# Attention output kept transposed up to the output projection, with the softmax division moved into the feed stage

## The reference, cut to what matters

```python
h = layernorm(x) * (1 + ca) + sa
q = h @ W_q;  k = h @ W_k;  v = h @ W_v
latent = (k + v) @ W_down_kv
k_rec, v_rec = latent @ W_up_k, latent @ W_up_v          # split in 16 heads
scores = q k_rec^T / 16 * exp(-0.01 |i - j|)
attn = softmax(scores);  out = attn @ v_rec              # heads joined to 256
x = x + ga * (out @ W_o)
h = layernorm(x) * (1 + cb) + sb
x = x + gb * fp4_linear(silu(fp4_linear(h, w_gate)) * fp4_linear(h, w_up), w_down)
```

## Time and profile before

| what | value |
|---|---|
| median of 3 runs | 2783.0 us (2781.36 to 2785.18) |
| span of the profiled execution, first to last instruction | 2775.7 us |
| PE / DVE / ACT / POOL busy, share of the span | 94% / 85% / 58% / 35% |
| mean granted TensorE clock | 0.940 of full |
| attention ends, feed setup ends, last instruction, about | at 2077, 2118 and 2776 us |

### The profile page before, as it was taken

How to read it: one execution, slowest core, us unless ns; L and a number is a source line. 1 busy time by engine, 2 the same in 40 slices (tenths; PEclk the granted TensorE clock), 3 DMA queues, 4 the chain that set the end, 5 groups by cost and what they waited for, 6 DMA issues and landing times. The chain is left out here.

```text
span 2775.7 us, 54634 instructions
## 1 busy us (share of the span) xinstructions
PE 2597.7 (94%) x15110; PEld 1209.7 (44%) x15110; DVE 2345.5 (85%) x4659; ACT 1601.3 (58%) x2988; POOL 970.2 (35%) x865
## 2 busy tenths in 40 slices
PE   5887679999999999999999999999978999999998
PEld 3333213343444444344344344443323566666665
DVE  5888698888888888888888888888756999999997
ACT  3666507777777777777777777777762222222221
POOL 3666522122122122122122122122231555555654
PEclk8767659999999999999999999999997999999999
DMA  4777864446455455455456455456201111111110
GB/s 152 246 247 255 265 129 73 71 74 99 62 85 87 63 82 82 71 78 86 70 78 86 72 80 86 69 79 94 39 11 38 37 41 40 40 40 42 40 32 18
DMA packets 207121, 238.56 MB, mean 86 GB/s; under 512 B 32256, under 2 KB 150784, under 8 KB 206720
## 3 DMA queue, kind: packets, MB, share of 16 engines
q1 hardware_dynamic: 194560, 218.56, 40.7%
q0 software_dynamic: 3072, 8.39, 1.2%
q10 hardware_dynamic: 9216, 8.39, 0.9%
HBM read 149.79 MB, written 83.89 MB: 84 GB/s over the span
## 5 line engine op out<-in xcount | busy, mean ns | idle before, releaser
L856 DVE CUSTOM_DVE_ANT_0 unread<-max_ps,toeplitz_sb 128x1024 bf16<-128x1024 f32 x1024 | 1219.2, 1219 | 230.5 <-PE max_ps L689 221.9
L817 ACT ACTIVATE probs<-score_ps 128x512 f32<-128x512 f32 x2048 | 1113.3, 597 | 438.3 <-PE score_ps L722 299.7
L689 PE MATMUL max_ps<-k_low,q_low 96*128 96x512 bf16 x2048 | 717.5, 393 | 30.0 <-DVE ident_bf L847 17.9
L651 POOL TENSOR_TENSOR probs<-probs,up_probs 128x512 f32<-128x512 f32 x256 | 336.8, 1316 | 624.4 <-ACT up_probs L821 624.4
L750 PE MATMUL pv_ps<-probs,v 128*32 128x512 f32 x4096 | 548.9, 608 | 3.4 <-POOL probs L651 3.4
L722 PE MATMUL score_ps<-q_low,k_low 99*128 99x512 bf16 (+3 forms) x1280 | 407.9, 320 | 4.9 <-ACT probs L817 4.1
L714 PE MATMUL score_ps<-q_up,k_up 99*128 99x512 bf16 (+3 forms) x1280 | 408.0, 319 | 4.5 <-ACT probs L817 3.8
L1284 PE MATMUL gu_ps<-wgu_t,turned 128*128 128x512 f32 (+1 forms) x768 | 314.7, 559 | 0.6 <-DVE hid L1445 0.6
L657 POOL DMA_DIRECT2D attn<-out_n x64 | 48.8, 762 | 698.3 <-DVE out_n L920 674.8
L714 PEld LDWEIGHTS score_ps<-q_up,k_up 99*128 99x128 bf16 x1280 | 123.8, 97 | 350.4 <-ACT probs L817 325.2
L689 PEld LDWEIGHTS max_ps<-k_low,q_low 96*128 96x128 bf16 x2048 | 194.0, 99 | 156.5 <-DVE row_max L856 83.9
(11 more groups left out here) (145 smaller groups left out, 3218.2 us busy)
## 6 DMA issues: line engine op xcount, KB each, us to landing
splits<-parts SPq DMA_DIRECT2D x128, 384.0 KB, 2.6
q_low<-splits SPq DMA_DIRECT2D x192, 128.0 KB, 4.4
k_low<-splits SPq DMA_DIRECT2D x192, 128.0 KB, 7.0
q_up<-splits SPq DMA_DIRECT2D x192, 128.0 KB, 9.4
k_up<-splits SPq DMA_DIRECT2D x192, 128.0 KB, 12.0
v_padded<-v_out SPq DMA_DIRECT2D x64, 256.0 KB, 3.5
v<-v_padded SPq DMA_DIRECT2D x32, 512.0 KB, 13.9
x_in<-in_L_attn_x SPq DMA_DIRECT2D x16, 512.0 KB, 4.6
```

Of the source, the lines that this page charges most:

```text
L651: nc.gpsimd.tensor_tensor(probs[:, g % PROBS, :, at:at + P], probs[:, g % PROBS, :, at:at + P], up_probs[:, g % 2], ALU.add).then_inc(diag ...
L689: mm = pe.matmul(max_ps[:, i % 2, half * HALF:(half + 1) * HALF], low[0][u][0:KROWS, h, qb * P:(qb + 1) * P], low[1][u][0:KROWS, h, half * ...
L817: nc.scalar.activation(probs[:, g % PROBS, h, :], score_ps[:, i % 2, :], ACT.Exp).then_inc(exp_done, 1)
L856: nc.vector.tensor_tensor_reduce(unread[:, i % 2, :], max_ps[:, i % 2, :], toeplitz[:, at:at + S], 1.0, -3.0e38, ALU.mult, ALU.max, row_ma ...
```

## The change

The attention output is no longer transposed and divided in the attention stage. ACT copies a finished half to one of two halves of `out_t`, and SP (not POOL) stores its 4 heads and its row sums, five DMAs, to `attn_t` (head, feature, token) and `sums`. `turn_out`, `invert_sums`, `normalise` and POOL's store go. In the feed setup the sums of all tokens are loaded, inverted on DVE in one operation over 128 x 1024 elements and stored to `inverse`. In the feed stage each tile loads its transposed attention (one DMA), the inverse sums spread over 16 feature rows each (two DMAs) and x; POOL multiplies the first two (`normalise_attention`, 128 x 256); PE projects the result directly. `turn_attention` goes, and ACT copies only the transposed input, 256 wide. PE's turning of the input waits only for its own buffers.

```diff
@@ attend_stage
-    out_t = sb("out_t", [P, HALF], F32)
-    inv_sum = sb("inv_sum", [P, DIAG, UH], F32)
-    out_n = sb("out_n", [P, DIAG, UH, HD], F32)
+    out_t = sb("out_t", [P, 2, HALF], F32)
...
+        def store_out(b, u, hf):
+            n = 2 * (UNITS * b + u) + hf
+            sp.wait_ge(out_copied, n + 1)
+            for h in range(UH):
+                sp.dma_start(t["attn_t"][b, u * UH + h, :, hf * HALF:(hf + 1) * HALF],
+                             out_t[h * VW:h * VW + HD, hf, :]).then_inc(out_stored[hf], 16)
+            sp.dma_start(t["sums"][b, u * UH:(u + 1) * UH, hf * HALF:(hf + 1) * HALF],
+                         out_t[HD:P:VW, hf, :]).then_inc(out_stored[hf], 16)
...
                 load_up(b if u < UNITS - 1 else b + 1, (u + 1) % UNITS)
+            if not (isinstance(unit, int) and unit == 0):
+                store_out(b if u > 0 else b - 1, (u - 1) % UNITS, 1)
+            store_out(b, u, 0)
+            if not (last and u == UNITS - 1):
                 load_max_rows(unit + 1, (u + 1) % UNITS)
...
-        def store(b, u, hf):
-            n = 2 * (UNITS * b + u) + hf
-            pool.wait_ge(out_ready, n + 1)
-            pool.dma_start(t["attn"][b, hf * HALF:(hf + 1) * HALF, u * UH * HD:(u + 1) * UH * HD].rearrange(
-                "(c p) n -> p c n", p=P), out_n[:].rearrange("p c h d -> p c (h d)")).then_inc(out_stored, 16)
...
-            if g == TILES + DIAG:
-                pe.wait_ge(out_ready, 2 * unit + 1)
+            if g == TILES + DIAG and not last:
+                pe.wait_ge(max_turn_copied, unit + 2)
...
-        def turn_out(n, turned_maxima=0):
...
-            for c in range(DIAG):
-                mm = pe.transpose(side_ps[:, c, :], out_t[:, c * P:(c + 1) * P], w["ident"][:])
-            mm.then_inc(out_turned, 1)
...
-        def copy_out(n):
-            act.wait_ge(pv_done, TILES * (n + 1))
-            act.wait_ge(out_turned, n)
-            nc.scalar.activation(out_t[:], pv_ps[:], ACT.Copy).then_inc(out_copied, 1)
+        def copy_out(unit, hf):
+            act.wait_ge(pv_done, TILES * (2 * unit + hf + 1))
+            if not (isinstance(unit, int) and unit == 0):
+                act.wait_ge(out_stored[hf], 16 * OUT_STORES * unit)
+            nc.scalar.activation(out_t[:, hf, :], pv_ps[:], ACT.Copy).then_inc(out_copied, 1)
...
-            nc.vector.reciprocal(inv_sum[:], turned[:, :, :, HD]).then_inc(inv_ready, 1)
...
-            nc.vector.tensor_tensor(out_n[:], turned[:, :, :, 0:HD],
-                                    inv_sum[:].unsqueeze(3).broadcast_to([P, DIAG, UH, HD]),
-                                    ALU.mult).then_inc(out_ready, 1)
@@ feed_setup_stage
+        sp.dma_start(sums[:], t["sums"].rearrange("b h s -> (b h) s")).then_inc(sums_loaded, 16)
         sp.dma_start(wo[:], t["wo"].rearrange("(k p) n -> p k n", p=P)).then_inc(wo_loaded, 16)
+        sp.wait_ge(sums_inverted, 1)
+        sp.dma_start(t["inverse"].rearrange("b h s -> (b h) s"), inverse[:]).then_inc(inverse_stored, 16)
+        sp.wait_ge(inverse_stored, 16)
...
+        dve.wait_ge(sums_loaded, 16)
+        nc.vector.reciprocal(inverse[:], sums[:]).then_inc(sums_inverted, 1)
+
         dve.wait_ge(wo_loaded, 16)
@@ feed_stage
-            sp.dma_start(attn_in[i % 4][:], t["attn"][b, i * P:(i + 1) * P, :]).then_inc(tile_loaded[i % 4], 16)
+            sp.dma_start(attn_in[i % 4][:], t["attn_t"][b, :, :, tokens].rearrange(
+                "(k h) d s -> (h d) k s", k=DC)).then_inc(tile_loaded[i % 4], 16)
+            heads = H // DC
+            for k in range(DC):
+                sp.dma_start(inverse_in[i % 4][:, k, :], t["inverse"][b, k * heads:(k + 1) * heads, tokens].unsqueeze(
+                    1).broadcast_to([heads, HD, P])).then_inc(tile_loaded[i % 4], 16)
             sp.dma_start(res_in[i % 4][:], t["x"][b, i * P:(i + 1) * P, :]).then_inc(tile_loaded[i % 4], 16)
...
-            pe.wait_ge(turned_copied, n + 1)
+            pe.wait_ge(attn_ready, n + 1)
             pe.wait_ge(x1_ready, n)
             for k in range(DC):
-                mm = pe.matmul(out_ps[:, 0:D], turned[i % 2][:, k, :], w["wo_g"][:, b, k, :],
+                mm = pe.matmul(out_ps[:, 0:D], attn[i % 2][:, k, :], w["wo_g"][:, b, k, :],
...
-        def turn_attention(b, i):
...
+        def normalise_attention(b, i):
+            n = TILES * b + i
+            count = held(pool, 16 * LOADS * ((TILES // 4) * b + i // 4 + 1))
+            if not (isinstance(b, int) and n < 2):
+                pool.wait_ge(projected, n - 1)
+            pool.wait_ge(tile_loaded[i % 4], count)
+            nc.gpsimd.tensor_tensor(attn[i % 2][:], attn_in[i % 4][:], inverse_in[i % 4][:],
+                                    ALU.mult).then_inc(attn_ready, 1)
...
                 inverse_std(*tile_at(b, i, NORM))
+            if tile_at(b, i, NORM_ATTENTION):
+                normalise_attention(*tile_at(b, i, NORM_ATTENTION))
             if tile_at(b, i, ROUND_INPUT):
```

More of the change, by code:

```diff
@@ L551, in attend_stage @@
     scores_ready, diag_added, pv_done = sem("scores_ready"), sem("diag_added"), sem("pv_done")
-    out_copied, out_turned, inv_ready, out_ready, out_stored = (
-        sem("out_copied"), sem("out_turned"), sem("inv_ready"), sem("out_ready"), sem("out_stored"))
+    out_copied = sem("out_copied")
+    out_stored = [sem(f"out_stored{i}") for i in range(2)]
     maxima_done, exp_done = sem("maxima_done"), sem("exp_done")
@@ L636, in _ @@
             step(B - 1, u, True)
+        store_out(B - 1, UNITS - 1, 1)
+        for i in range(2):
+            sp.wait_ge(out_stored[i], 16 * OUT_STORES * UNITS * B)
     @block.gpsimd
@@ L652, in add_diagonal, with unit_steps @@
                                     up_probs[:, g % 2], ALU.add).then_inc(diag_added, 1)
-        def store(b, u, hf):
-            n = 2 * (UNITS * b + u) + hf
-            pool.wait_ge(out_ready, n + 1)
-            pool.dma_start(t["attn"][b, hf * HALF:(hf + 1) * HALF, u * UH * HD:(u + 1) * UH * HD].rearrange(
-                "(c p) n -> p c n", p=P), out_n[:].rearrange("p c h d -> p c (h d)")).then_inc(out_stored, 16)
-        def unit_steps(b, u, first):
+        def unit_steps(b, u):
             for g in range(DIAG):
                 add_diagonal(b, u, g)
-            if not first:
-                store(*steps_back(b, u, 0, 1)[:2], 1)
-            store(b, u, 0)
             for g in range(TILES + DIAG, STEPS):
@@ L669, in _ @@
         for u in range(UNITS):
[L670 removed]
+            unit_steps(0, u)
         with pool.Fori(1, B) as b:
             for u in range(UNITS):
[L673 to L675 removed]
+                unit_steps(b, u)
     @block.tensor
@@ L775, in unit_steps @@
                     if h == 1 and is_diagonal(g):
-                        up_diagonals(b, u, g)
+                        up_diagonals(b, u, g, last)
                 if not (first and g < LAG):
                     values(*steps_back(b, u, g, LAG))
-                if g == 5 and not first:
-                    turn_out(2 * unit - 1)
                 if g == 9 and not last:
                     turn_maxima(unit + 1)
-                if g == 10:
-                    turn_out(2 * unit, 0 if last else unit + 2)
         def max_tiles(u, n):
@@ L832, in unit_steps @@
                 if g == 1 and not first:
-                    copy_out(2 * unit - 1)
+                    copy_out(unit - 1, 1)
                 if g == TILES + 1:
-                    copy_out(2 * unit)
+                    copy_out(unit, 0)
         for u in range(UNITS):
@@ L931, in unit_steps @@
                         maxima(ahead[0], ahead[1], ahead[2] + i)
-                    if not first and (g, i) == (6, 0):
-                        invert_sums(2 * unit - 1)
-                    if not first and (g, i) == (6, 1):
-                        normalise(2 * unit - 1)
                     if not last and (g, i) in SPLIT_AT:
@@ L1022, in feed_setup_stage @@
     wo = sb("wo", [P, DC, D], F32)
+    sums = sb("sums", [P, S], F32)
+    inverse = sb("inverse", [P, S], F32)
     row_ps = st.enter_context(nc.psum_tensor("row_ps", [P, 2, 2, HALF], F32))
@@ L1158, in sem @@
         return st.enter_context(nc.semaphore(name))
-    attn_in = [sb(f"attn_in{i}", [P, D], F32) for i in range(4)]
+    attn_in = [sb(f"attn_in{i}", [P, DC, P], F32) for i in range(4)]
+    inverse_in = [sb(f"inverse_in{i}", [P, DC, P], F32) for i in range(4)]
+    attn = [sb(f"attn{i}", [P, DC, P], F32) for i in range(2)]
     res_in = [sb(f"res_in{i}", [P, D], F32) for i in range(4)]
-    turned = [sb(f"turned{i}", [P, 2 * DC, P], F32) for i in range(2)]
+    turned = [sb(f"turned{i}", [P, DC, P], F32) for i in range(2)]
     x1 = [sb(f"x1_{i}", [P, D], F32) for i in range(TILES)]
```

81 lines of the change are left out of this document (27 added, 54 removed).

## The result

The changed kernel takes 2804.8 us (median of four executions, 2803.2 to 2811.1), the kernel before in the same comparison 2782.2. The ratio is 1.009 with a 95% interval of 1.0072 to 1.0108: 22.6 us slower, where the prediction had 5.9 slower and a range that ended at 2804. The profiled execution of the changed kernel is the longest of its four (span 2809.3 us), 33.6 us above the span before.

What follows compares the result with a forecast made beforehand. The prediction took PE's transposes to be on attention's path and a POOL-DVE ring to pace feed. Its terms, -30.9 - 0.7 + 1.4 + 5.9 + 30.2 = +5.9 us, took 2783.0 to 2788.9 us; range 2757 to 2804.

Steps and rivals of the forecast that it cites:

- What bounds the stages: Attention: PE's transposes are on the path, 0.49 us a step; feed: POOL and DVE alternate, 9.60 us an iteration.
- Feed's ring of GpSimd and VectorE: Feed iteration: 2.4 us of POOL and 7.1 us of DVE, each waiting for the other, make 9.6 us.
- Attention, taken off: Attention: removing `turn_out` from PE saves 0.49 us at each of 63 places in the loop, 30.9 us less.
- if half of it fell to other engines: Attention: lower bound for the gain from removing the transposes, 15 us instead of the whole 30.9.
- Attention, added: Attention: SP's five DMA issues for each half, 2.1 us a half, are hidden by later steps; cost 0.
- the attention gain doesn't come: Attention: rival in which SP's queue or ACT's wait on a store replaces the gain; 2820 us, chance 0.05.
- End of attention: Attention's end: the last of five store issues starts sooner after ACT's copy, 0.7 us less with unchanged landing.
- The inversion: Feed setup: DVE inverts 1024 elements in 6.7 us, so the gating starts 1.4 us later.
- Filling: Feed's start: first projection 0.7 us late, then links of 4.9 us through POOL's queue; 5.9 us more.
- Feed, added: Feed: POOL's multiply holds DVE 0.53 us in each of 57 tight iterations, 30.2 us more.
- whole instruction: Feed: rival in which DVE loses, or POOL comes late by, 0.72 us a tile; +16.7, 2799.7 us, chance 0.09.
- no hold: Feed: rival in which POOL's multiply doesn't delay DVE and iterations stay 9.60 us; -24.3, 2758.7 us, chance 0.13.

Runs made afterwards that it cites:

- the one with the spread instructions: Changed kernel plus 72 waiting TensorE instructions ahead of the attention loop, spread behind its first 32 maxima tiles; 2784.0 us, ratio 1.0009.
- the early run: Changed kernel with GpSimd's feed division 0.7 us earlier, right behind `var_eps`, and `rstd` moved behind it; 2803.1 us, ratio 1.0086.
- the late one: Changed kernel with GpSimd's feed division 2.2 us later, waiting for VectorE's seventh step on the hidden tile; 2800.9 us, ratio 1.0074.

## Why the prediction missed

- *What bounds the stages:* right. Feed's ring of GpSimd and VectorE at 9.60 us was the pace; without hold and without transposes it is 9.60 again, not 9.35.
- *Attention, taken off (-30.9):* this is the step that failed, in the words "I take the whole". The gain of a step came (0.45 us a group over a unit, 0.49 in the step shown), and with the loop head moved the 31 units are 31.0 us shorter. As the change was made, they were 4.7 us shorter in the profiled execution, and 8.7 to 10.5 in the five later variants with the same attention code: removing instructions ahead of the loop moved its head to where PE runs out of instructions a second time, 3.6 to 4.3 us five times, with the clock at half speed around it. The earlier trace rows show a step that doesn't cross the loop's end; I multiplied its 0.49 over all units and never looked at the five units that cross it, of which the trace before already showed 54 to 58 us in place of 50.8. The same paragraph named 15 us "if half of it fell to other engines", but the bound entered neither the sum nor the range; with it the sum would have been near the measured 2804.8, by luck, since no other engine took over. Between the changed kernel (2804.8) and the one with the spread instructions (2784.0) lie 20.8 us, or about 18 if each is taken against the kernel before of its own comparison, and 2784.0 is 4.5 above its kernel before, where the sum said 5.9. So but for this stop the sum holds, in part by luck: of the 31.0 us the 26 other units gave 21.7, where 0.98 each would be 25.5, and the five at the loop heads 9.3 instead of 4.9.
- *Attention, added (0):* right. No wait of PE for a load stands among its waits in attention, so no store held up the row maxima. The rival "the attention gain doesn't come" named the outcome that came closest to what happened in this stage, for a cause that wasn't there, SP's queue; its 2820 is 15 us above the measured time.
- *End of attention (-0.7):* the last stretch is 3.2 shorter, of which 0.5 is a transpose group; 2 us better than predicted. The way from the end of ACT's copy to the last issue is 0.6 shorter, as predicted. The prediction took the landing as unchanged, but the next stage begins 2.2 us behind that issue, where it was 3.4, and ACT's copy comes earlier too, for which no cause was looked for. SP's timeline in the changed kernel:

```profile
2071.01 0.52 SPq L608 DMA_DIRECT2D sums_dram<-out_t  x1
2073.18 0.36 SPq L1002 DMA_DIRECT2D sums<-sums_dram  x1
```

- *The inversion (+1.4):* 6.54 us against 6.7, and feed setup 0.7 longer. Right within its bounds. The estimate of 8.5 us from the repeat count in the Trainium skill (VectorE: DVE Perf Modes, walkthrough) is not what the trace shows.
- *Filling (+5.9):* +7.3. The links were right (4.86 against 4.9); the first projection came 1.6 us later after the stage's start instead of 0.7.
- *Feed, added (+30.2):* +29.8, with `h_buf` at 0.82 as said. The 57 iterations were not quite alike: one in eight lasted 11.03 us before and the next 9.82, and this last one grew by 0.31 only. The rival "whole instruction" (0.72) and "no hold" are both refuted by the same row.

## What to carry to other kernels

A gain measured on a step in the middle of an unrolled loop has to be checked at the loop's head too, where the engine jumps: list the "issue" waits there, before and after, and if a new one appears, move the loop head by a few dozen idle instructions, put where the engine waits anyway. GpSimd's idle time beside a busy VectorE is not free for work on SBUF: moving the operation only moved the wait between the two, and here VectorE did the work itself for less than it lost by the help.

## What the hardware showed that I had not expected

A satisfied wait on PE isn't free in a row: 72 instructions of two waits each delayed the stage by 5.5 us, 189 by 22.6, so some 0.1 us each (the mark itself moves between 391 and 396 us without them); spread where PE waits for VectorE they cost nothing that shows (first transpose of maxima at 394.9 us, in the changed kernel 395.0).

Which of the two engines waits is not settled by the kind of operation. GpSimd's multiply, begun during VectorE's L954 `h_buf`, stopped the `tensor_tensor` behind it (1.42 us); begun during L960 `h_buf`, it was itself kept out over three operations (1.98 us). Both times an operation of VectorE was running when it began. The Trainium skill (SBUF — State Buffer, "Who interferes with whom") lets the order of issue decide and counts a VectorE operation with two SBUF inputs among those that contend. The trace agrees on the second. On the first it does not settle it: GpSimd's record begins 0.23 us ahead of `hid_buf` in the early run and 0.17 ahead in the late one, and only in the early run did it go first. Why, no run here shows.
